# Moving the store of v and the load of the gate from the SyncE queue to the ScalarE queue in a fused state-space layer

## The reference, cut to what matters

```python
def _L0_attn_ref(x, W_in, b_in, W_conv, b_conv, W_x, b_x, W_out, b_out, A_log, D):
    xr = x @ W_in.T + b_in
    xi, res = jnp.split(xr, 2, axis=-1)
    xc = conv(xi)  # depthwise, 4 taps, causal
    xi = silu(xc)
    proj = xi @ W_x.T + b_x
    delta = jax.nn.softplus(proj[..., :DI])
    B_ssm, C_ssm = proj[..., DI:DI + N], proj[..., DI + N:]
    dA = jnp.exp(delta[..., None] * -jnp.exp(A_log))
    dBx = delta[..., None] * B_ssm[:, :, None, :] * xi[..., None]
    # h = dA * h + dBx over time, y = sum over n of h * C
    y = scan(...) + xi * D
    y = y * silu(res)
    return y @ W_out.T + b_out

xn = _layernorm(x)
s = _L0_attn_ref(xn, ...)
g = _silu(_L0_ffn_ref(xn, ...))   # ternary weights
x = x + s * g
```

## Time and profile before

| what | us |
|---|---|
| three timed runs, median | 13609.37 |
| their range | 13367.98 to 13653.0 |
| profiled execution, its own time | 13431.25 |
| span of its slowest core (core 4) | 13429.7 |
| spans of the other cores | 13092.5 to 13345.0 |
| VectorE busy on core 4 | 7594.2 (57%) |
| TensorE busy on core 4 | 5986.5 (45%) |
| ScalarE busy on core 4 | 2736.6 (20%) |

### The profile page before, as it was taken

One profiled execution on the slowest core, in us unless ns is written; L12 is line 12 of the kernel. 1 busy time (PEld: TensorE's weight loads), 2 busy tenths in 40 slices (PEclk: granted clock), 3 DMA queues, 4 the chain that ended last, 5 costly groups with the idle time before them and its releaser, 6 DMA issues.

```text
span 13429.7 us, 82652 instructions; the slowest of 8 cores (13092.5 to 13429.7 us)
## 1 busy us (share of the span) xinstructions
PE 5986.5 (45%) x21004; PEld 4097.4 (31%) x21004; DVE 7594.2 (57%) x10669; ACT 2736.6 (20%) x6342; POOL 7.2 (0%) x17
## 2 busy tenths in 40 slices
PE   4625252424242434334343333333333301887887
PEld 3524142323232323233333333322333200333333
DVE  1157585858484848484848484848484887001000
ACT  1112121312131313131313121212121221000000
POOL 0000000000000000000000000000000000000000
PEclk9867676767676767666667777676767655787778
DMA  3313232222222222222222222222222201112221
GB/s 110 111 54 90 58 89 60 85 63 83 65 82 66 81 67 75 73 73 75 74 75 71 78 71 78 71 77 71 77 72 74 69 24 53 70 65 85 69 72 63
DMA packets 546575, 979.42 MB, mean 73 GB/s; under 512 B 61091, under 2 KB 291059, under 8 KB 546102
## 3 DMA queue, kind: packets, MB, share of 16 engines
q1 hardware_dynamic: 435078, 873.15, 21.0%
q10 hardware_dynamic: 110592, 100.71, 3.5%
q0 software_dynamic: 432, 0.28, 0.0%
HBM read 855.93 MB, written 117.96 MB: 73 GB/s over the span
## 4 chain that ended last, share of the span: by engine, by line
DVE 39%; PE 33%; DMA 15%; ACT 5%; issue 4%; SPq 3%; DVEq 1%; ACTq 0%; POOL 0%; POOLq 0%
DVE p_h L818 14%; PE pb L433 10%; PE pb L792 10%; DMA p_wo<-w_in_t 9%; PE pb L1082 8%; DVE p_dz L811 7%; DVE p_dz L826 6%; DVE p_y L831 6%; PE pb L1090 4%; DMA wx<-w_x_t 3%; DVE p_cv L559 3%; DMA p_x<-x 1%; SPq L690 1%; SPq L644 1%; DMA v_s<-p_y 1%
## 5 line engine op out<-in xcount | busy, mean ns | idle before, releaser
L792 PE MATMUL pb<-p_xi,wx 128*128 128x256 f32 (+1 forms) x8704 | 2055.7, 393 | 4801.3 <-DMA wx<-w_x_t 4631.5
L792 PEld LDWEIGHTS pb<-p_xi,wx 128*128 128x128 f32 (+1 forms) x8704 | 1615.4, 191 | 5240.5 <-issue 5025.9
L818 DVE TENSOR_TENSOR_SCAN p_h<-p_da,hstate,p_dz 128x256 f32<-128x256 f32 x4096 | 2741.7, 732 | 109.5 <-DVE p_dz L811 3.7
L611 ACT ACTIVATE p_da<-p_del,ca 128x256 f32<-128x256 f32 x4096 | 1730.4, 498 | 4082.0 <-DVE p_h L818 4081.2
L433 PE MATMUL pb<-p_xnf,p_wo 128*128 128x256 f32 x8192 | 2162.1, 419 | 815.1 <-DMA p_wo<-w_in_t 545.2
L433 PEld LDWEIGHTS pb<-p_xnf,p_wo 128*128 128x128 f32 x8192 | 1641.7, 209 | 1335.3 <-issue 1099.0
L811 DVE TENSOR_TENSOR p_dz<-p_dtx,p_bcb 128x1024 f32<-128x1024 f32 x1024 | 1255.1, 1226 | 674.4 <-ACT p_da L611 437.6
L873 DVE TENSOR_SCALAR p_y<-p_xi,cdv 128x256 f32<-128x256 f32 x256 | 68.7, 350 | 2323.9 <-DMA v_s<-p_y 2323.8
L831 DVE TENSOR_TENSOR p_y<-p_y,p_dz 128x1024 f32<-128x1024 f32 x1024 | 1254.5, 1225 | 110.3 <-DVE p_dz L826 4.6
L826 DVE TENSOR_TENSOR p_dz<-p_h,p_bcb 128x1024 f32<-128x1024 f32 x1024 | 1255.0, 1226 | 109.2 <-DVE p_h L818 3.2
L1082 PE MATMUL pb<-p_v,wo 128*128 128x512 f32 x2048 | 1019.5, 668 | 21.5 <-DMA wo<-w_out_t 21.5
(11 more groups left out here) (87 smaller groups left out, 1808.0 us busy)
## 6 DMA issues: line engine op xcount, KB each, us to landing
p_wo<-w_in_t SPq DMA_DIRECT2D x1056, 256.0 KB, 2.8
wx<-w_x_t SPq DMA_DIRECT2D x256, 768.0 KB, 4.4
wx<-w_x_t SPq DMA_DIRECT2D x256, 272.0 KB, 2.7
p_x<-x SPq DMA_DIRECT2D x128, 512.0 KB, 7.8
p_bcb<-bc_s ACTq DMA_DIRECT2D x512, 128.0 KB, 4.0
wo<-w_out_t SPq DMA_DIRECT2D x128, 512.0 KB, 3.3
sres_s<-p_s ACTq DMA_DIRECT2D x256, 128.0 KB, 2.2
xi_s<-p_s SPq DMA_DIRECT2D x256, 128.0 KB, 1.8
```

What stands on the lines that cost most here:

```text
L611: li = s.activation(out=da[:, t_i * TP:(t_i + 1) * TP], in_=sdel[jj % 2][:, t_i * TP:(t_i + 1) * TP], func=AF.Exp, scale=ca[:, t_i * NS + ...
L792: li = t.matmul(dst, wxb[k % 2][:, lc:lc + w], xi2[:, k * TP:(k + 1) * TP], start=st_, stop=sp_)
L818: li = v.tensor_tensor_scan(out=h_all[:, (t_i % 8) * TP:(t_i % 8 + 1) * TP], data0=da[:, t_i * TP:(t_i + 1) * TP], data1=dz[:, (t_i - tp_) ...
```

## The change

The load of `srs` and the store of `sy_` leave SyncE's stream and go into ScalarE's, behind dA 14 and 15 of chunk j-1 and ahead of the copies of P1 of chunk j+1. The store now comes first and the load second; both keep their semaphores and what they wait for. The store of the last chunk (j = 15) goes to ScalarE too, behind all of that chunk's dA. Nothing is computed otherwise.

```diff
                 if j + 1 < NC2:
                     emit_winloads(j + 1, ckT)
 
-                @blk.sync
-                def _(sy, j=j, prev=prev):
-                    if j >= 1:
-                        p.wait(sy, "cv", prev[3] + 262)
-                    for par in range(2):
-                        p.wait(sy, f"qt{par}", S["store_qtb"][j][par] + 128)
-                    for t_i in range(DT_I):
-                        p.inc(sy.dma_start(out=srs[:, t_i * TP:(t_i + 1) * TP],
...
-                              "qr", 16)
-                if prev is not None:
-                    @blk.sync
-                    def _(sy, j=j, prev=prev):
-                        p.wait(sy, "cv", prev[3] + 262)
...
-                            p.inc(sy.dma_start(
-                                out=v_d[:, t_i * T + jp * TP: t_i * T + jp * TP + TP],
...
                     emit_dA_part(j - 1, [14, 15], daB, prev[3], prev_qbs,
                                  prevcv_prev)
                 qb_j = (p.c["qb0"], p.c["qb1"])
+
+                @blk.scalar
+                def _(s, j=j, prev=prev):
+                    if prev is not None:
+                        p.wait(s, "cv", prev[3] + 262)
+                        jp = j - 1
+                        for t_i in range(DT_I):
+                            p.inc(s.dma_start(
+                                out=v_d[:, t_i * T + jp * TP: t_i * T + jp * TP + TP],
+                                in_=sy_[:, t_i * TP:(t_i + 1) * TP]), "qv", 16)
+                    for par in range(2):
+                        p.wait(s, f"qt{par}", S["store_qtb"][j][par] + 128)
+                    for t_i in range(DT_I):
+                        p.inc(s.dma_start(
+                            out=srs[:, t_i * TP:(t_i + 1) * TP],
+                            in_=sres_d[:, t_i * T + j * TP: t_i * T + j * TP + TP]),
+                              "qr", 16)
 
                 if j + 1 < NC2:
                     emit_p1_evacs(j + 1, ckT)
```

More of the change, by code:

```diff
@@ L670, in build_nc @@
                     emit_winloads(j + 1, ckT)
-                @blk.sync
-                def _(sy, j=j, prev=prev):
-                    if j >= 1:
-                        p.wait(sy, "cv", prev[3] + 262)
-                    for par in range(2):
-                        p.wait(sy, f"qt{par}", S["store_qtb"][j][par] + 128)
-                    for t_i in range(DT_I):
-                        p.inc(sy.dma_start(out=srs[:, t_i * TP:(t_i + 1) * TP],
-                                           in_=sres_d[:, t_i * T + j * TP: t_i * T + j * TP + TP]),
-                              "qr", 16)
-                qt0_sres = p.c["qr"]
-                if prev is not None:
-                    @blk.sync
-                    def _(sy, j=j, prev=prev):
-                        p.wait(sy, "cv", prev[3] + 262)
-                        jp = j - 1
-                        for t_i in range(DT_I):
-                            p.inc(sy.dma_start(
-                                out=v_d[:, t_i * T + jp * TP: t_i * T + jp * TP + TP],
-                                in_=sy_[:, t_i * TP:(t_i + 1) * TP]), "qv", 16)
-                qt1_vst = p.c["qv"]
                 daB = csb
@@ L761, in build_nc @@
                 qb_j = (p.c["qb0"], p.c["qb1"])
+                @blk.scalar
[14 more added lines that the diff above has]
+                              "qr", 16)
+                qt0_sres = p.c["qr"]
+                qt1_vst = p.c["qv"]
                 if j + 1 < NC2:
@@ L903, in build_nc, with _ @@
                 if j == NC2 - 1:
-                    @blk.sync
-                    def _(sy, j=j, cvb=cvb):
-                        p.wait(sy, "cv", cvb + 262)
+                    emit_dA_part(j, list(range(NS)), csb + (6 if j == 0 else 262),
+                                 cvb, qbs_j, prevcv_prev)
+                    @blk.scalar
+                    def _(s, j=j, cvb=cvb):
+                        p.wait(s, "cv", cvb + 262)
                         for t_i in range(DT_I):
-                            p.inc(sy.dma_start(
+                            p.inc(s.dma_start(
                                 out=v_d[:, t_i * T + j * TP: t_i * T + j * TP + TP],
                                 in_=sy_[:, t_i * TP:(t_i + 1) * TP]), "qv", 16)
-                    emit_dA_part(j, list(range(NS)), csb + (6 if j == 0 else 262),
-                                 cvb, qbs_j, prevcv_prev)
         with contextlib.ExitStack() as es3:
```

## The result

| | before | changed |
|---|---|---|
| median of ten runs, us | 13528.43 | 14009.9 |
| range | 13261.09 to 13775.07 | 13874.85 to 14191.42 |
| span of the slowest core in the profile | 13429.7 (core 4) | 13873.0 (core 3) |
| core 4 in the same profile | 13429.7 | 13714.1 |

The change makes the kernel slower. The reported ratio is 1.0595, with a 95% interval of 1.043 to 1.076. It compares only undisturbed runs, those in which the granted clock of neither group of four cores (0 to 3, 4 to 7) had fallen behind, and of 14 listed executions of the changed kernel one was such a run, 13710.84 us.

What follows compares the result with a forecast made beforehand. Bound by a ring of scans, the rest of P1, then the next scans; 13431.25 + 512 (fourteen turns) + 7.5 - 3.9 = 13,947, or 14,125 on the median; 14,000 predicted, range 13,700 to 14,250.

Steps and rivals of the forecast that it cites:

- a third of the way between the two: Whole kernel: 14,000 chosen between 13,947 on the profiled execution's time and 14,125 on the median of the runs shown.
- The wait for the store goes, gain 14.4 a turn: VectorE at line 873, between chunks: the store's excess delay before the first product vanishes, gaining 14.4 us a turn.
- The wait costs ScalarE its lead of 33.0: ScalarE before P1's copies: waiting for VectorE's end of line 894 costs 33.0 us a turn, covered by nothing.
- 32 issues, 16.5, and 1.5 for hand-over and table: ScalarE ahead of P1: DMA issues, semaphore and activation table put the first copy 18.0 us after VectorE's end.
- Contention costed at nothing: During P1's transposes: 4 MB in 32 DMAs move while TensorE needs no weights, costing nothing.
- The turn, + 36.6: Each of the 14 loop turns holding a P1: + 33.0 + 18.0 - 14.4 = + 36.6 us, + 512 in all.
- Chunk 0, + 7.5: Iteration 0: 16 load issues stand ahead of P1 of chunk 1, on which the first scans wait, costing 7.5 us.
- Chunk 14 to 15, - 3.9: Last turn, with no P1 following: the product starts at 10854.7 against 10858.62, gaining 3.9 us.
- P1 gets its clock back: TensorE in P1: longer rest restores full clock, P1 177 instead of 193.4 us, time about 13,720; chance 0.08.
- The issues cost nothing: ScalarE ahead of P1: DMA issues are free, a turn costs 20.1 us, time 13,709; chance 0.03.
- Not slower, P1 closes its gaps: TensorE between P1's weight tiles: waits vanish, P1 151 us, a turn - 5.8, time about 13,350; chance 0.05.
- The queue backs up: ScalarE's DMA issues: store takes 19.36 us instead of 9.05, adding 10.3 a turn, time 14,090 and more; chance 0.12.

Runs made afterwards that it cites:

- the repeats: Both kernels unedited, profiled again: changed kernel twice, medians 14019.59 (ratio 1.032) and 14068.53 (1.033); kernel before once, 13631.89.
- e4: Kernel before with store and load on GpSimd's queue, plus ScalarE's bare wait for line 894's end ahead of P1's copies; median 13849.9, ratio 1.020.
- e3: Kernel before with store and load moved to GpSimd's queue instead of ScalarE's, same waits; median 13466.71, ratio 0.992.
- e8: GpSimd version of the kernel before, with the gate's load also waiting for state n = 2 of its chunk's scans; median 13337.44, ratio 0.973.
- e7: Changed kernel with the same bytes in 4 + 4 DMAs of 512 KB instead of 16 + 16 of 128 KB; median 13965.27, ratio 1.019.
- e5: Kernel before with only the store of v moved to ScalarE ahead of P1's copies, load left on SyncE; median 13964.43, reported ratio 1.0349.

## Why the prediction was right or wrong

The direction and the mechanism were right, and the time came out: 14,000 was forecast and 14,009.9 measured. The size of the change was wrong as stated. "I predict 14,000, a third of the way between the two" is the step that failed. The working gave + 516 on 13,431, or 3.8%. By mixing a sum on the profiled execution with the median of three runs I gave away a quarter of it: 14,000 stands 2.9% above the 13,609 I had. The medians of ten runs show 3.6% and the repeats 3.2 and 3.3%. So the sum was about right. That the time hit is luck: the base taken was 81 us above the median that the kernel before had over ten runs, and the share of the sum that was given away made up for it. The reported 5.95% is under-forecast by half. That number stays open: none of the turns, parts or medians above shows a term of its size, and six runs over seven, above, give 4.0%.

Point by point:

- *The wait for the store goes, gain 14.4 a turn.* Right in kind. It was read on core 4; over all cores "to product" fell from 22.5 and 23.0 to 6.0, so the gain was 17. Core 2, where the store once took 19.36 us to issue, and core 3, with up to 19.7, gained more. The 6.0 us floor from chunk 0 held, by a lucky choice of core: on core 4 the first product of chunk 0 did start 6.0 us after B's issue, on the other seven 11.3 to 18.0.
- *The wait costs ScalarE its lead of 33.0.* Right to the tenth, and e4 alone shows it.
- *32 issues, 16.5, and 1.5 for hand-over and table.* 18.0 forecast, 17.3 measured: 15.4 for the issues, 0.1 for the start, 1.3 for the table and 0.3 between them.
- *Contention costed at nothing.* Right for the changed kernel and for a reason I named only in half: the transfers run while ScalarE issues and P1 stands still. Where all 4 MB were allowed beside P1 they cost 5 to 6 us a turn (e3, e4), and the store's 2 MB alone cost 3 (e8).
- *The turn, + 36.6.* On core 4 it was + 35.1 (680.4 to 715.5), over the cores + 34.7 in the first two profiles and + 30.5 over all five. Of the overshoot of 6.1, 2.4 is the store's gain, mis-sized by reading one core, and 0.7 the start of P1 (50.3 instead of 51.0). The other 3 are P1 and the scans, 1.7 and 1.1 shorter, which is within their spread. On core 4 the signs named beforehand held: P1 was 190.3, 187.4 and 193.2 in the three profiles, inside 187 to 200.
- *Chunk 0, + 7.5.* Wrong in sign. The first scans began at 805.8 instead of 823.5 us. The issues did stand ahead of P1, but the gate's load no longer ran into B's: "to product" fell from 13.7 to 7.7 there. For the rest, P1's first copy came 6.4 us earlier and P1 was 5.3 shorter. On core 4 P2 of chunk 0 ended 5 us earlier on TensorE (its last stretch ran from 594.61 to 599.60 before and ended at 594.76 after), and the issues then held ScalarE for 6.5. The repeats give 822.7 before, 809.1 and 811.6 after.
- *Chunk 14 to 15, - 3.9.* 27.4 to 22.8 us from VectorE's end to the first product, - 4.6.

The rivals. *P1 gets its clock back*: it rested 98 instead of 47 us, and the late stretch of P1 shows the same granted clock as the earlier trace rows:

```profile
5592.00:5636.00 44.00, 33.35 (x130) 25.39 (x131) 0.00 (x0) 3.14 (x8) 0.00 (x0) 0.94 0.32 95
5724.00:5774.00 50.00, 36.04 (x119) 26.59 (x117) 0.00 (x0) 2.55 (x7) 0.00 (x0) 0.78 0.38 106
```

0.78 against 0.77, and P1 was 186.4 against 188.1, a difference smaller than the 5.7 between the two profiles of the kernel before. The 16 us a turn that this rival needed are not there. *The issues cost nothing*: e4 against the changed kernel shows 15.8 us of ScalarE's time. The Trainium skill's statement that the sequencer's time is usually small beside the DMA (DMA: Bandwidth & Descriptors, "Issuing engines are not separate DMA queues") doesn't hold for these thirty-two: the store's sixteen took 7.9 us to issue, and the last of them landed 1.7 us later. That all issuing engines share the same DMA engines, from the same section, fits e3, where transfers from GpSimd's queue stretched the steps fed by SyncE's weight loads from 21.9 to 26.1 us. *Not slower, P1 closes its gaps*: the waits for weight tiles fell from 545 to 477 us on core 4, 5 a turn and far from the 37 needed. *The queue backs up*: no; in the three profiles of the changed kernel the store's 16 issues took at most 9.4 us on any core and the load's at most 10.5, where the store's had taken up to 19.7 before. Why it took so long there no run shows.

## What to carry to other kernels

Before a DMA with a wait is moved to another engine, ask what stands behind it in that engine's stream and how far that engine runs ahead: here the lead of 33 us was worth twice the store's delay of 17. Put such a transfer on a queue with nothing behind it, and place it in time by what else wants the DMA engines then. And make a sum and its base from the same execution: a forecast change in per cent is lost if the time is moved to another base afterwards.

## What was not expected of the hardware

- An issue on ScalarE cost 0.48 us for 128 KB and 0.9 us for 512 KB (e7), so fewer, larger DMAs halve the issue time but don't quarter it.
- 4 MB moved beside P1's weight loads stretched P1 by 5 to 6 us (e3, e4), in just the steps in which they moved. The DMA engines' share, 0.35 to 0.39 in P1 before, was 0.75 in that stretch of e3, so they were not full on average. But each tile is loaded only when its buffer falls free, and then 5.8 us over the 16 tiles of two steps, 0.4 us a tile, are all on the path.
- B's broadcast load of 128 KB, on which the scans start, brought the first product 6 us after its issue when alone and 12.5 with the gate's 2 MB just ahead of it (e5).
